# Shifting the copies of transposed probabilities by one slot and spreading the projections over the slots of a fused attention kernel

## The chip, the cores and the metric

The kernel runs on one core of a Trainium2 chip. The metric is device time in microseconds. The engines are TensorE (PE), VectorE (DVE), ScalarE (ACT), GpSimd (POOL) and the SP queue, which issues most DMAs. Each engine runs its own list of instructions in order and meets the others only at semaphores.

## What is computed

Sixteen images of 256 rows by 256 columns go through a small fixed filter and give 256 tokens each; 77 text tokens per image are looked up in a table, so that each batch item has S = 333 tokens of width 256. Two residual blocks follow, windowed attention with 16 heads of width 16 and a mixture of 8 experts with 2 chosen for each token:

```python
h = concatenate([filter(x), table[x_txt]], axis=1)            # [16, 333, 256]
h = h + attention(layernorm(h))   # windows of 128 at 0, 64, 128, 192 and 205, position bias
                                  # softmax, average over the windows that cover a token, Wo
h = h + experts(layernorm(h))     # softmax gate, top 2 of 8, SwiGLU of width 512, weighted sum
```

## The kernel before

The program has two stages. The first runs `run_steps` (L291): a step for each b from -2 to 17, and in it every engine runs the same Python loop `for k in range(G)` with G = 20 slots, that is 5 windows of 4 groups, a group being 4 heads. A step works at once on five batch items in different states (`has`, L310): attention of item b (`att`), the end of attention, output projection, gate and second layernorm of item b-1 (`tail`), expert places and scatter of item b-2 (`tail2`), projections of item b+1 (`proj`), image and text loads of item b+2 (`inp`). The second stage (`run_tiles`, L296) runs the experts over sorted tiles of rows; it starts when the first is over, and its code is the same before and after.

What each engine does in slot k of the first stage, in this order:

- TensorE (L1042 on): scores of group k (4 bf16 products, L1052); transposes of the probabilities of group k-3 (L1063); product with the values for group k-4 (8 instructions, L1079); in slots 0, 4, 8, 12, 16 the transposes of `raw` (L1089), the output rows of a window; in slots 2, 6, 10, 14, 18 the transposes of `ctx_q` (L1097). Then the other work of that slot: slot 0 transposes of the normalised input (L1108), slot 1 the prefix counts (L1115), slots 2 to 5 one projection of q or k each (L1132), slots 8 and 9 the output projection (L1030), slot 11 all three projections of v (L1037), slot 16 transposes of the normalised rows (L1163), slot 18 the gate (L1170).
- ScalarE (L633 on): four Exp of group k-1 (L640); the copy of the transposed probabilities of group k-2 out of PSUM into `probsT` (L653), for three groups in four; in slots 3, 7, ... the copy `raw` (L660); in slots 2, 6, ... the copy `head_out` (L667); last the evacuations of the projections: `xT` in slot 0 (L672), q and k in slots 2 to 5 (L684), `x2T` in slot 16 (L691).
- VectorE (L775 on): score plus bias with row minimum for group k (L783); in slots 3, 7, ... the copy of group k-2, whose number in its window is `DVE_G` (L792); in slots 1, 5, ... reciprocals and `ctx_q` (L804, L811); and small work of the layernorms, the gate, the bf16 parts of q and k (`part_high`, L757, `part_middle`, L764), v with bias (`add_v`, L771), residual (L889), normalise (L738), two bit masks of the image differences (L878).
- GpSimd (L517 on): image differences (L540, L552), their sum and clip (L544, L549), the window sums (L527), the remaining bf16 parts (L507, L514), six indirect stores (L498), inverse roots for the layernorms (`inverse_roots`, L473), copies and residual.
- SP (L334 on): for the next item, writes of the bf16 parts to DRAM and loads of them back as stacks (L365, L372), in one fixed order; then the shifts of v (L396 to L400), which wait for `add_v`; then the image loads of the next step (L342 to L346).

The buffers that couple the engines are two deep for `s_bank` (scores), `t_bank` (transposed probabilities in PSUM) and `probsT`, four deep for `probs`. TensorE's transposes into a `t_bank` buffer wait for the copy of two groups before (L1061). The projections share `m_bank`, so that the q and k products of one half wait for the evacuation of the product before in it (L1128).

## Time and profile before

| | |
|---|---|
| median of 3 runs | 1393.93 us (1393.73 to 1397.23) |
| profiled execution | 1392.94 us, span 1390.1 us |
| TensorE busy in the span | 1172.4 us (84%) |
| VectorE busy | 847.6 us (61%) |
| ScalarE busy | 710.9 us (51%) |
| GpSimd busy | 590.6 us (42%) |
| first stage with attention | about 60 to 830 us, 16 batch items |
| expert stage | about 870 to 1390 us |

Times in the profile are microseconds from the start of the span. A share of busy time over the whole span mixes the two stages, so the first stage is read by itself, in seven steps from 403.7 to 738.9 us in which every kind of work is present. An idle time is shown with the instruction that came after it and with the one that ended it.

### The profile page before, as it was taken

The page shows a single profiled execution, that of the slowest core. Times are in us where ns is not written, and L with a number is a line of the kernel's source. Part 1 is how long each engine was busy: PE and PEld are TensorE (multiplying, and loading weights), DVE is VectorE, ACT ScalarE, POOL GpSimd, SP SyncE. Part 2 cuts the span into 40 slices and gives each one's busy share as a digit, 9 for nine tenths or more (in the row PEclk, how much of TensorE's full clock was granted, in tenths as well). Part 3 has the DMA queues.
Part 4 walks back from the last instruction along what each step waited for, and adds up shares of the span by engine and source line. Part 5 has one row for each costly group of instructions (what it writes and reads, how often), then busy time and mean ns, then how long its engine had stood idle before and what let it go on. Part 6 is the DMA issues. An engine that isn't in the chain of part 4 may idle for free.

```text
span 1390.1 us, 34367 instructions
## 1 busy us (share of the span) xinstructions
PE 1172.4 (84%) x10510; PEld 964.1 (69%) x10511; DVE 847.6 (61%) x4259; ACT 710.9 (51%) x1976; POOL 590.6 (42%) x750
## 2 busy tenths in 40 slices
PE   1366888788888888888888872999999999999996
PEld 1244666566666666666666551999999999999995
DVE  4364777877777777878877764344444444444442
ACT  0185878877788788788778870211111111111111
POOL 5443365546546554654564334232322232223222
PEclk9698999999999999999999995999999999999998
DMA  3694464366336444633653307232232333232322
GB/s 111 148 240 92 98 146 88 88 126 131 78 94 141 102 88 111 146 80 86 136 122 64 86 28 229 38 51 46 49 47 48 49 45 49 46 49 46 49 45 34
DMA packets 98394, 123.31 MB, mean 89 GB/s; under 512 B 15544, under 2 KB 87416, under 8 KB 95192
## 3 DMA queue, kind: packets, MB, share of 16 engines
q1 hardware_dynamic: 75880, 89.96, 29.1%
q0 software_dynamic: 18576, 24.47, 10.9%
q10 hardware_dynamic: 3808, 7.34, 1.8%
q8 instruction: 59, 0.97, 0.3%
q14 instruction: 71, 0.58, 0.2%
HBM read 69.35 MB, written 46.07 MB: 83 GB/s over the span
## 4 chain that ended last, share of the span: by engine, by line
PE 65%; ACT 17%; DVE 6%; issue 6%; DMA 4%; POOL 2%; SPq 1%; another core or an unknown queue 0%; ACTq 0%; DVEq 0%; POOLq 0%
PE s_bank L1196 12%; PE t_bank L1196 12%; PE o_bank L1211 11%; ACT probs L640 8%; PE t_bank L1063 6%; PE m_bank L1132 4%; PE m_bank L1030 3%; DMA qk_parts<-parts_flat 3%; PE s_bank L1052 3%; PE o_bank L1089 3%; PE o_bank L1079 3%; PE m_bank L1037 3%; ACT raw L660 2%; ACT probsT L653 2%; DVE probs L783 1%
## 5 line engine op out<-in xcount | busy, mean ns | idle before, releaser
L640 ACT ACTIVATE probs<-probs,neg_max 128x128 f32<-128x128 f32 x1280 | 407.0, 397 | 6.9 <-DVE neg_max L783 6.8
L783 DVE CUSTOM_DVE_ANT_0 probs<-s_bank,nbias 128x128 f32<-128x128 f32 x1280 | 293.5, 285 | 72.2 <-PE s_bank L1052 68.1
L653 ACT ACTIVATE probsT<-t_bank 128x512 f32<-128x512 f32 x240 | 142.2, 593 | 136.4 <-PE t_bank L1063 122.4
L1063 PE MATMUL t_bank<-ident,probs 128*128 128x128 f32 x1280 | 203.8, 284 | 3.8 <-ACT probs L640 3.5
L705 ACT ACTIVATE v_all<-s_bank 128x512 f32<-128x512 f32 x91 | 54.4, 598 | 286.5 <-PE s_bank L1196 276.6
L1211 PE MATMUL o_bank<-stacks,v_all 128*128 x728 | 172.4, 380 | 0.6 <-issue 0.3
L1052 PE MATMUL s_bank<-stacks 96*128 96x128 bf16 x1280 | 130.9, 226 | 48.4 <-DMA stacks<-qk_parts 37.6
L1052 PEld LDWEIGHTS s_bank<-stacks 96*128 96x128 bf16 x1280 | 93.5, 101 | 94.2 <-DMA stacks<-qk_parts 38.3
L617 POOL DMA_INDIRECT out_dram<-wq_sb,nbias x46 | 74.8, 1627 | 193.1 <-DVE wq_sb L985 171.8
L617 POOL DMA_INDIRECT out_dram<-wk_sb,nbias x45 | 73.6, 1635 | 176.4 <-DVE wk_sb L985 173.6
L1063 PEld LDWEIGHTS t_bank<-ident,probs 128*128 128x128 f32 x1280 | 141.8, 147 | 7.1 <-ACT probs L640 7.0
L1079 PE MATMUL o_bank<-probsT,v_all 128*32 128x128 f32 x2560 | 139.5, 290 | 6.2 <-ACT head_out L667 5.7
L1211 PEld LDWEIGHTS o_bank<-stacks,v_all 128*128 128x128 f32 x728 | 131.3, 190 | 15.6 <-issue 1.5
L991 DVE TENSOR_TENSOR v_all<-v_all,t_bank 128x512 f32<-128x512 f32 x91 | 62.6, 688 | 128.6 <-PE t_bank L1196 128.6
L792 DVE COPY probsT<-t_bank 128x512 f32<-128x512 f32 x80 | 55.2, 691 | 105.1 <-PE t_bank L1063 104.6
L498 POOL DMA_INDIRECT expert_slots<-rows,slot_i x96 | 96.0, 1000 | 46.7 <-issue 38.2
L699 ACT ACTIVATE v_all<-m_bank 128x256 f32<-128x256 f32 x91 | 34.9, 383 | 143.0 <-PE m_bank L1185 143.0
L783 DVE DVE_READ_ACCUMULATOR2_ANT neg_max<- 128x1 f32 x1280 | 105.0, 82 | 0.0
L1089 PE MATMUL o_bank<-ident,raw 128*128 128x128 f32 x320 | 53.5, 290 | 55.7 <-ACT raw L660 55.4
L1079 PEld LDWEIGHTS o_bank<-probsT,v_all 128*32 128x32 f32 x2560 | 52.0, 109 | 64.0 <-issue 50.8
L1196 PEld LDWEIGHTS s_bank<-v_all,probs 128*128 128x128 f32 x736 | 91.0, 195 | 3.2 <-ACT v_all L699 0.9
L1196 PE MATMUL s_bank<-v_all,probs 128*128 128x128 f32 x736 | 91.4, 278 | 0.5 <-ACT v_all L699 0.5
(159 smaller groups left out, 2065.3 us busy)
## 6 DMA issues: line engine op xcount, KB each, us to landing
stacks<-qk_parts SPq DMA_DIRECT2D x192, 166.5 KB
qk_parts<-parts_flat SPq DMA_DIRECT2D x192, 83.2 KB
nbias<-expert_slots SPq DMA_DIRECT2D x91, 129.0 KB
w_sb<-in_L_ffn_w_dram ACTq DMA_DIRECT2D x14, 512.0 KB
v_all<-v_all SPq DMA_DIRECT2D x64, 96.0 KB, 3.4
x_here<-in_x_dram SPq DMA_DIRECT2D x16, 256.0 KB, 3.0
out_dram<-h_res SPq DMA_DIRECT2D x16, 256.0 KB
stacks<-in_L_ffn_w_dram SPq DMA_DIRECT2D x8, 512.0 KB
```

The source lines that it names most:

```text
L498: pool.indirect_dma_start(slots_dram[:, :], bass.IndirectOffsetOnAxis(slot_i[0:n, kk, j:j + 1], 0), rows[0:n, kk, j, :], None).then_inc(sc ...
L617: pool.indirect_dma_start(out[:, :], bass.IndirectOffsetOnAxis(g_rows[r][:, D + 1:D + 2].bitcast(I32), 0), y_sb[r], None, compute_op=ALU.a ...
L640: ins = act.activation(seg, seg, ACT.Exp, bias=neg_max[:, r, i:i + 1], scale=-1.0)
L653: act.activation(probsT[:, k % 2, :], t_bank[:, k % 2, :], ACT.Copy).then_inc(pT_by_act, 1)
L783: ins = dve.tensor_tensor_reduce(probs[:, r, i * WIN:(i + 1) * WIN], s_bank[:, k % 2, i * WIN:(i + 1) * WIN], nbias[:, h, :], 1.0, BIG, AL ...
L991: dve.tensor_tensor(hidT[r % 2], hidT[r % 2], t_bank[:, r % 2, :], ALU.mult).then_inc(hid_ready, 1)
L1052: mm = pe.matmul(s_bank[:, k % 2, i * WIN:(i + 1) * WIN], q_stack[par][0:KROWS, h, lo:lo + WIN], k_stack[par][0:KROWS, h, lo:lo + WIN], st ...
L1063: mm = pe.transpose(t_bank[:, (k - 3) % 2, i * WIN:(i + 1) * WIN], probs[:, r, i * WIN:(i + 1) * WIN], ident[:, :])
L1079: mm = pe.matmul(o_bank[32 * i:32 * i + 32, vp, g * WIN:(g + 1) * WIN], v_win[bp][:, w, c0:c0 + 2 * HD], probsT[:, (k - 4) % 2, i * WIN:(i ...
L1089: mm = pe.transpose(o_bank[:, vp, g * WIN:(g + 1) * WIN], raw[:, g * WIN:(g + 1) * WIN], ident[:, :])
L1196: mm = pe.matmul(bank[:, par, n * P:(n + 1) * P], up_w[par][:, m, a, n * P:(n + 1) * P], gxT[par][:, a * P:(a + 1) * P], start=(a == 0), s ...
L1211: mm = pe.matmul(o_bank[:, r % 2, 0:D], hidT[r % 2][:, a * P:(a + 1) * P], w2_sb[:, bass.ds(e, 1), a, :].rearrange("p o n -> p (o n)"), st ...
```

## The change

The copies of `probsT` move by one slot on ScalarE and VectorE: slot k now copies group k-3 instead of k-2, and VectorE's share is the group with number 3 of a window instead of 1, so that it copies in slots 2, 6, 10, 14, 18. TensorE's products with the values stay where they are. On TensorE the `raw` transposes go to the very end of their slot, the q and k projections are given out as six pieces over slots 2 to 6, the output projection over slots 8 to 10, the v projections over slots 11 to 14, the gate over slots 17 and 18, and the prefix counts go from slot 1 to 2. On ScalarE the evacuations stand first in a slot: `xT` in slot 1, q and k in slots 3, 4, 6, 7, `x2T` in slot 17. VectorE and GpSimd have their small work moved to fit: the second layernorm's statistics in slot 12, roots in 13, normalise in 15 (before: 11, 12, 14); `add_v` in 14 and 15 (12, 13); `part_high(1)` in slot 7 (6) and `part_middle(0)` in 6 (7); the image differences both in slot 0 (2, 3), both masks in slot 1 (2, 4), sum and clip in slot 2 (6).

```diff
-DVE_G = 1
+DVE_G = 3
...
-                    if inp and k == 2:
+                    if inp and k == 0:
...
                         pool.tensor_tensor(diag[:, :, :], x_here[:, :, 0:IMG], x_below[:, :, 1:IMG + 1],
                                            ALU.subtract).then_inc(diffs_ready, 1)
-                    if inp and k == 6:
+                    if inp and k == 0:
+                        pool.tensor_tensor(anti[:, :, :], x_below[:, :, 0:IMG], x_here[:, :, 1:IMG + 1],
+                                           ALU.subtract).then_inc(diffs_ready, 1)
+                    if inp and k == 2:
...
                         pool.tensor_tensor(diag[:, :, :], diag[:, :, :], anti[:, :, :], ALU.add).then_inc(conv_step, 1)
...
-                    if inp and k == 3:
-                        pool.tensor_tensor(anti[:, :, :], x_below[:, :, 0:IMG], x_here[:, :, 1:IMG + 1],
-                                           ALU.subtract).then_inc(diffs_ready, 1)
...
-                    if (tail or inp) and k == 12:
+                    if (tail or inp) and k == 13:
...
-                    if tail and k == 15:
+                    if tail and k == 16:
...
+                    if proj and k == 1:
+                        act.wait_ge(xT_done, b1 + 1)
+                        if b1 >= 1:
+                            act.wait_ge(v_done, b1 * 2)
+                        act.activation(xT[:, :, :], m_bank[:, :, 0:S], ACT.Copy).then_inc(xT_ready, 1)
+                    if proj and k in (3, 4, 6, 7):
+                        n, c = {3: (0, 0), 4: (0, 1), 6: (1, 0), 7: (1, 1)}[k]
+                        act.wait_ge(qk_done, b1 * 4 + 2 * n + c + 1)
+                        if b1 >= 1:
+                            act.wait_ge(rest_ready, b1 * 2)
+
+                        act.activation(qk[:, 2 * n + c, :], m_bank[:, c, 0:S], ACT.Identity,
+                                       bias=(bq_col if n == 0 else bk_col)[:, c:c + 1],
+                                       scale=(-SCALE if n == 0 else 1.0)).then_inc(qk_ready, 1)
+                    if tail and k == 17:
+                        act.wait_ge(x2T_done, b0 + 1)
+                        if proj:
+                            act.wait_ge(part3_ready, b1 * 2 + 2)
+                        act.activation(x2T[:, :, :], m_bank[:, :, 0:S], ACT.Copy).then_inc(x2T_ready, 1)
...
-                    g = (k - 2) % NG
-                    if g != DVE_G and ((k >= 2 and att) or (k < 2 and tail)):
-                        n = b * G + (k - 2)
+                    if (k - 3) % NG != DVE_G and ((k >= 3 and att) or (k < 3 and tail)):
+                        n, r = b * G + (k - 3), (k - 3) % 2
                         act.wait_ge(pT_done, n + 1)
                         if n >= 2:
                             act.wait_ge(pv_done, n - 1)
-                        act.activation(probsT[:, k % 2, :], t_bank[:, k % 2, :], ACT.Copy).then_inc(pT_by_act, 1)
+                        act.activation(probsT[:, r, :], t_bank[:, r, :], ACT.Copy).then_inc(pT_by_act, 1)
...
-                    if tail2 and k == 1:
+                    if tail2 and k == 2:
...
                         ins.then_inc(max_ready, 1)
-                    if (k - 2) % NG == DVE_G and ((k >= 2 and att) or (k < 2 and tail)):
-                        n = b * G + (k - 2)
+                    if (k - 3) % NG == DVE_G and ((k >= 3 and att) or (k < 3 and tail)):
+                        n, r = b * G + (k - 3), (k - 3) % 2
                         dve.wait_ge(pT_done, n + 1)
                         if n >= 2:
                             dve.wait_ge(pv_done, n - 1)
-                        dve.tensor_copy(probsT[:, k % 2, :], t_bank[:, k % 2, :]).then_inc(pT_by_dve, 1)
...
                     if proj and k == 6:
+                        part_middle(0)
+                    if proj and k == 7:
                         part_high(1)
-                    if proj and k == 7:
-                        part_middle(0)
-                    if inp and k in (2, 4):
-                        dve.wait_ge(diffs_ready, b2 * 2 + k // 2)
-                        bits = (diag, anti)[k // 2 - 1][:, :, :].bitcast(I32)
-                        dve.tensor_scalar(bits, bits, 0x7FFFFFFF, None, ALU.bitwise_and).then_inc(conv_step, 1)
+                    if inp and k == 1:
+                        for i, side in enumerate((diag, anti)):
+                            dve.wait_ge(diffs_ready, b2 * 2 + i + 1)
+                            bits = side[:, :, :].bitcast(I32)
+                            dve.tensor_scalar(bits, bits, 0x7FFFFFFF, None, ALU.bitwise_and).then_inc(conv_step, 1)
...
                         moments_of(h_in[par], stats1, 0, b2, ln1_step)
-                    if tail and k == 10:
-                        dve.wait_ge(wo_done, b0 * 2 + 2)
+                    if tail and k in (10, 11):
+                        dve.wait_ge(wo_done, b0 * 2 + k - 9)
                         dve.wait_ge(res_ready, b0 + 1)
...
-                    if tail and k == 11:
+                    if tail and k == 12:
...
-                    if proj and k == 12:
+                    if proj and k == 14:
...
-                    if proj and k == 13:
+                    if proj and k == 15:
                         add_v(2, 4)
-                    if tail and k == 14:
+                    if tail and k == 15:
...
+                def qk_proj(n, c, a):
+                    mm = pe.matmul(m_bank[:, c, 0:S], (wq_sb if n == 0 else wk_sb)[:, a, c * P:(c + 1) * P],
+                                   xT[:, a, :], start=(a == 0), stop=(a == C - 1))
+                    if a == C - 1:
+                        mm.then_inc(qk_done, 1)
+
+                def v_proj(bank, o, w, a):
+                    mm = pe.matmul(m_bank[:, bank, o:o + D], xT[:, a, STARTS[w]:STARTS[w] + WIN],
+                                   wv_sb[:, a, :], start=(a == 0), stop=(a == C - 1))
+                    if w and a == C - 1:
                         mm.then_inc(v_done, 1)
 
...
-                    v = (k - 5) // NG
-                    if (k - 5) % NG == 3 and ((att and v >= 0) or (tail and v < 0)):
...
+                    if tail2 and k == 2:
...
-                    if proj and k in (2, 3, 4, 5):
...
+                    if proj and k == 2:
+                        pe.wait_ge(xT_ready, b1 + 1)
+                        qk_proj(0, 0, 0)
+                        qk_proj(0, 0, 1)
+                    if proj and k == 3:
+                        if tail2:
                             pe.wait_ge(prefix_read, b9 * 2 + 2)
...
+                        qk_proj(0, 1, 0)
+                        qk_proj(0, 1, 1)
+                    if proj and k == 4:
+                        pe.wait_ge(qk_ready, b1 * 4 + 1)
+                        qk_proj(1, 0, 0)
+                    if proj and k == 5:
+                        qk_proj(1, 0, 1)
+                        pe.wait_ge(qk_ready, b1 * 4 + 2)
+                        qk_proj(1, 1, 0)
+                    if proj and k == 6:
+                        qk_proj(1, 1, 1)
...
                     if tail and k == 9:
                         out_proj(1)
+                    if tail and k == 10:
...
                     if proj and k == 11:
                         pe.wait_ge(qk_ready, b1 * 4 + 4)
                         if tail:
+                            pe.wait_ge(h2_ready, b0 * NT + 2)
+                        v_proj(0, 0, 0, 0)
+                        v_proj(0, 0, 0, 1)
+                    if proj and k == 12:
+                        v_proj(0, D, 2, 0)
+                    if proj and k == 13:
+                        v_proj(0, D, 2, 1)
+                        if tail:
                             pe.wait_ge(h2_ready, b0 * NT + NT)
-                        v_proj(0, 0, 0)
-                        v_proj(0, D, 2)
-                        v_proj(1, 0, 4)
+                        v_proj(1, 0, 4, 0)
+                    if proj and k == 14:
+                        v_proj(1, 0, 4, 1)
                     if tail and k == 16:
                         pe.wait_ge(rows0_ready, b0 * 3 + 3)
                         if proj:
...
-                    if tail and k == 18:
+                    if tail and k in (17, 18):
                         pe.wait_ge(x2T_ready, b0 + 1)
-                        for j, (t0, n) in enumerate(TILES):
+                        for j in ((0, 1), (2,))[k - 17]:
...
+                        if k == 18:
+                            mm.then_inc(logits_done, 1)
+                    v = (k - 5) // NG
+                    if (k - 5) % NG == 3 and ((att and v >= 0) or (tail and v < 0)):
+                        wv, vp = b * NW + v, (par + v) % 2
+                        pe.wait_ge(raw_ready, wv + 1)
+                        for g in range(NG):
+                            mm = pe.transpose(o_bank[:, vp, g * WIN:(g + 1) * WIN], raw[:, g * WIN:(g + 1) * WIN],
+                                              ident[:, :])
+                        mm.then_inc(rawT_done, 1)
```

## Rows read from the trace of the kernel before

**Rows 1.** Seven batches: busy us of PE, PEld, DVE, ACT, POOL (count), clock, DMA.

```profile
451.40:498.40 47.00, 39.69 (x421) 28.67 (x420) 37.72 (x246) 38.80 (x114) 26.55 (x38) 1.00 0.52 110
498.40:547.80 49.40, 42.74 (x421) 30.91 (x419) 37.58 (x242) 38.60 (x113) 26.44 (x38) 0.93 0.48 105
...
sum 335.20, PE 287.76 PEld 207.44 DVE 263.73 ACT 271.08 POOL 184.15; mean PE 41.11 PEld 29.63 DVE 37.68 ACT 38.73 POOL 26.31
```

**Rows 2.** Groups by line, 403.7 to 738.9 us: busy, mean ns, idle before, releasers.

```profile
L640 ACT ACTIVATE probs<-probs,neg_max 128x128 f32<-128x128 f32 x562 | 178.8, 397 | 3.7 <-DVE neg_max L783 3.7
L783 DVE CUSTOM_DVE_ANT_0 probs<-s_bank,nbias 128x128 f32<-128x128 f32 x563 | 129.2, 285 | 21.5 <-PE s_bank L1052 20.9 <-issue 0.4
...
L653 ACT ACTIVATE probsT<-t_bank 128x512 f32<-128x512 f32 x105 | 62.3, 593 | 53.9 <-PE t_bank L1063 49.4 <-issue 2.8 <-remote 1.5
...
L1052 PE MATMUL s_bank<-stacks 96*128 96x128 bf16 x560 | 57.5, 227 | 5.8 <-DVE neg_max L783 5.8
...
L1089 PE MATMUL o_bank<-ident,raw 128*128 128x128 f32 x142 | 23.8, 290 | 22.2 <-ACT raw L660 22.1
L1079 PEld LDWEIGHTS o_bank<-probsT,v_all 128*32 128x32 f32 x1120 | 22.7, 109 | 27.7 <-issue 22.5 <-ACT probsT L653 5.2
...
L1097 PE MATMUL o_bank<-ident,ctx_q 128*128 128x128 f32 x70 | 16.6, 321 | 7.6 <-DVE ctx_q L811 7.6
```

**Rows 3.** Waits, 403.7 to 738.9 us: who waited for whom, total, times, longest.

```profile
PE m_bank L1115 <- ACT xT L672: 7.3, 7, 1.0
```

**Rows 4.** Chain around slot 16 of one batch: start us, us, what.

```profile
488.81 0.60 ACT raw L660
...
490.92 0.44 PE t_bank L1063 x4
```

**Rows 5.** Timeline of ScalarE, 489 to 540 us: start us, us, operation, idle before.

```profile
491.89 0.72 ACT L691 ACTIVATE rest<-m_bank 128x666 f32<-128x666 f32 x1
...
520.98 0.60 ACT L653 ACTIVATE probsT<-t_bank 128x512 f32<-128x512 f32 x1 [2.75 <-issue]
```

**Rows 6.** Timeline of TensorE, 480 to 545 us: start us, us, operation, idle before.

```profile
494.15 0.39 PE L1052 MATMUL s_bank<-stacks 96*128 96x128 bf16 x4
...
494.91 0.43 PE L1079 MATMUL o_bank<-probsT,v_all 128*32 128x128 f32 x8
495.26 0.40 PE L1052 MATMUL s_bank<-stacks 96*128 96x128 bf16 x4
...
525.75 2.83 PE L1037 MATMUL m_bank<-wv_sb,xT 128*128 128x256 f32 x12
...
539.38 0.74 PE L1163 MATMUL m_bank<-ident,rows 128*128 128x128 f32 x6
...
544.69 0.40 PE L1052 MATMUL s_bank<-stacks 96*128 96x128 bf16 x4
```

**Rows 7.** Timeline of VectorE, 521.9 to 548 us: the normalise of slot 14.

```profile
535.35 1.06 DVE L738 TENSOR_SCALAR rows<-h_res,moments,rstd 128x256 f32<-128x256 f32 x3
```

**Rows 8.** Timeline of GpSimd, 489 to 541 us: a difference, the last root step.

```profile
498.27 1.10 POOL L540 TENSOR_TENSOR diag<-x_here,x_below 128x512 f32<-128x512 f32 x1
...
535.02 0.20 POOL L489 TENSOR_TENSOR rstd<-rstd,root_tmp 128x6 f32<-128x6 f32 x1
```

**Rows 9.** VectorE's L818 over the span: ns min/median/max, first and last start.

```profile
L818 DVE TENSOR_TENSOR below_best<-best x16: 178/954/990, 163.4 to 852.5; 128x24 f32<-128x24 f32 x16
```

**Rows 10.** Chain of the first attention batch: start us, us, what.

```profile
87.01 14.14 DMA qk_parts<-parts_flat
...
114.02 0.61 PE s_bank L1052 x4
```

**Rows 11.** Timeline of SP's queue, 490 to 600 us: last stack load, next image.

```profile
533.72 0.31 SPq L372 DMA_DIRECT2D stacks<-qk_parts  x1
...
538.76 0.44 SPq L345 DMA_DIRECT2D x_below<-in_x_dram  x1
```

**Rows 12.** The page's part 6: DMA issues, KB each, us to landing.

```profile
x_here<-in_x_dram SPq DMA_DIRECT2D x16, 256.0 KB, 3.0
```

More of the change, by code:

```diff
@@ L791, in step @@
                             dve.wait_ge(pv_done, n - 1)
-                        dve.tensor_copy(probsT[:, k % 2, :], t_bank[:, k % 2, :]).then_inc(pT_by_dve, 1)
+                        dve.tensor_copy(probsT[:, r, :], t_bank[:, r, :]).then_inc(pT_by_dve, 1)
                     v = (k - 6) // NG
@@ L1033, in out_proj @@
                         mm.then_inc(wo_done, 1)
-                def v_proj(bank, o, w):
-                    for a in range(C):
-                        mm = pe.matmul(m_bank[:, bank, o:o + D], xT[:, a, STARTS[w]:STARTS[w] + WIN],
-                                       wv_sb[:, a, :], start=(a == 0), stop=(a == C - 1))
-                    if w:
+                def qk_proj(n, c, a):
[7 more added lines that the diff above has]
+                    if w and a == C - 1:
                         mm.then_inc(v_done, 1)
@@ L1083, in step @@
                         mm.then_inc(pv_done, 1)
-                    v = (k - 5) // NG
-                    if (k - 5) % NG == 3 and ((att and v >= 0) or (tail and v < 0)):
-                        wv, vp = b * NW + v, (par + v) % 2
-                        pe.wait_ge(raw_ready, wv + 1)
-                        for g in range(NG):
-                            mm = pe.transpose(o_bank[:, vp, g * WIN:(g + 1) * WIN], raw[:, g * WIN:(g + 1) * WIN],
-                                              ident[:, :])
-                        mm.then_inc(rawT_done, 1)
+                    if tail2 and k == 2:
+                        pe.wait_ge(taken_ready, b9 + 1)
+                        if proj:
+                            pe.wait_ge(xT_ready, b1 + 1)
+                        pe.matmul(counted[:, 0:NT * E], before[:, :], taken[:, :, :].rearrange("p j e -> p (j e)"),
+                                  start=True, stop=False, skip_group_check=True)
+                        for j in range(NT):
+                            mm = pe.matmul(counted[:, (j + 1) * E:(NT + 1) * E].rearrange("p (r e) -> p r e", e=E),
+                                           ones[:, :], taken[:, j:j + 1, :].to_broadcast([P, NT - j, E]),
+                                           start=False, stop=(j == NT - 1), skip_group_check=True)
+                        mm.then_inc(prefix_done, 1)
                     v = (k - 7) // NG
@@ L1109, in step @@
                         mm.then_inc(xT_done, 1)
-                    if tail2 and k == 1:
-                        pe.wait_ge(taken_ready, b9 + 1)
-                        if proj:
-                            pe.wait_ge(xT_ready, b1 + 1)
-                        pe.matmul(counted[:, 0:NT * E], before[:, :], taken[:, :, :].rearrange("p j e -> p (j e)"),
-                                  start=True, stop=False, skip_group_check=True)
-                        for j in range(NT):
-                            mm = pe.matmul(counted[:, (j + 1) * E:(NT + 1) * E].rearrange("p (r e) -> p r e", e=E),
-                                           ones[:, :], taken[:, j:j + 1, :].to_broadcast([P, NT - j, E]),
-                                           start=False, stop=(j == NT - 1), skip_group_check=True)
-                        mm.then_inc(prefix_done, 1)
@@ L1123, in step @@
[L1123 to L1134 removed]
+                    if proj and k == 2:
+                        pe.wait_ge(xT_ready, b1 + 1)
+                        qk_proj(0, 0, 0)
+                        qk_proj(0, 0, 1)
@@ L1171, in step @@
                                                start=(a == 0), stop=(a == C - 1))
-                        mm.then_inc(logits_done, 1)
+                        if k == 18:
[8 more added lines that the diff above has]
+                        mm.then_inc(rawT_done, 1)
             run_steps(step)
```

32 lines of the change are left out of this document (3 added, 29 removed).

## Prediction

> **What bounds the kernel now.** I read the table of engines by stretch first, for the attention stage alone. Over seven batches of 335.2 us in all, 47.9 us a batch, TensorE is busy 41.1 us, ScalarE 38.7 and VectorE 37.7 [rows 1]. No engine is full: TensorE idles 6.8 us a batch, ScalarE 9.2, VectorE 10.2. Three engines with nearly equal loads run in lists that are coupled through two-deep buffers, and what is lost is lost in waits for each other, so the kernel is bound by the order of work and not by one engine. A batch has 20 slots, 2.4 us each on average. A slot with attention work alone starts 1.11 us after the one before on TensorE, while slot 11 carries 2.83 us of v projections at once [rows 6]. ScalarE's four Exp and a copy take 318 x 4 + 593 ns = 1.87 us at most (178.8 us over 562 Exp is 318 ns) in every slot [rows 2]. So TensorE waits in the bare slots and ScalarE in the full ones, because only about one slot of work fits between them.
>
> The groups by line then say where TensorE waits in these seven batches: 22.2 us before the `raw` transposes (L1089), 7.6 us before the `ctx_q` transposes (L1097), 5.8 us before the scores (L1052) [rows 2], and 7.3 us before the prefix counts, for `xT` [rows 3]. ScalarE waits 53.9 us before its copies of `probsT`, nearly all for the transposes of L1063 [rows 2].
>
> The chain shows that the two are one loop. ScalarE issues `raw` at 488.81 us (0.60 us), TensorE stands until that is done, then does the `raw` transposes, the six transposes of slot 16, scores, and only then the transposes that end at 491.36 [rows 4], for which ScalarE's next copy was waiting. ScalarE has had 1.2 us of Exp to do in between and idles for the rest. Slots 0, 4, 8 and 16 have such a stretch of other work behind the `raw` transposes; in slot 8 of that batch ScalarE idled 2.75 us [rows 5].
>
> **The change, part by part.** The batch is the unit; gains and losses are in us a batch.
>
> `raw` transposes last in their slot. They now stand behind 0.45 to 1.0 us of projections or transposes, and ScalarE issues `raw` right behind the copy for which the product of L1079 waits. The wait of 22.2 / 7 = 3.17 goes [rows 2]. What is late next: `ctx_q` on VectorE a slot later, which has TensorE's whole next slot as cover.
>
> `xT` evacuated in slot 1 and first used in slot 2, prefix counts in slot 2. The wait of 7.3 / 7 = 1.04 goes [rows 3]. ScalarE now waits for transposes that TensorE did at the end of the slot before; its copy of that slot (593 ns) covers most of them.
>
> Projections spread. The 2.83 us of slot 11 [rows 6] become pieces over four slots, and statistics, residual and `add_v` on VectorE are spread too. The waits for VectorE (L1097 and L1052) are (7.6 + 5.8) / 7 = 1.9 [rows 2]. They come from bunches of small work, of which the change undoes some and makes one new. I count half, 0.96; bounds 0 and 1.9. Sum of gains 3.17 + 1.04 + 0.96 = 5.17.
>
> Copies one slot later. Between TensorE and ScalarE the loop stays one slot long: before, slot k of ScalarE needed transposes of slot k+1 and fed the product of slot k+2; now those of slot k, for the product of slot k+1. What is gained is that the transposes no longer wait for the Exp right behind the copy. What is lost is a slot between scores and product: Exp of group k now has to be over before the copy of group k-2. ScalarE's waits turn into waits of TensorE before L1079. Today TensorE's weight loads there wait 5.2 / 7 = 0.74 for the copy [rows 2]. In the bare slots (1, 7, 15, 19) ScalarE is the slower engine, so part of the 3.17 has to come back. Bounds: 0 and the whole 3.17. I take 1.1, nearer the 0.74, since that is the same wait.
>
> Normalise one slot later (slot 15), used by TensorE in slot 16. Today it starts at 535.35, lasts 1.06 us and ends 3.0 us before the transposes of 539.38 [rows 6, 7]; the last root step ends at 535.22 [rows 8], so it can't start earlier relative to the statistics. A slot is 2.4 us, so 0.6 us of cover is left on average. Loss between 0 and 1.06; I take 0.3.
>
> Gate from slot 17 on. `x2T` (0.72 us, [rows 5]) now stands first in ScalarE's slot 17 and TensorE's gate of the same slot needs it; TensorE has only the product of L1079 (0.35 us from 494.91 to 495.26, [rows 6]) beside it. Loss 0.72 - 0.35 = 0.4, bounds 0 and 0.72.
>
> VectorE's slots 0 to 2. They hold the choice of experts, both masks and now the copy of `probsT`, and GpSimd's two image differences stand beside them. A small VectorE operation on 128x24 values (L818) takes 954 ns in the median against 178 at least; it starts at the time of GpSimd's 1.10 us difference [rows 8, 9]. With two differences in a row a second operation can be held up in that way: bounds 0 and 2 x 0.78 = 1.6 for the slowest chain; I take 0.6, since part of it hides behind ScalarE. The image itself must be there by slot 0: its load follows the shifts of v in SP's queue, which wait for `add_v`, now two slots later. Today it is issued by 538.76 and lands 3.0 us later [rows 11, 12], 2.9 us ahead of the next step's first scores at 544.69 [rows 6]; two slots (4.8 us) later it lands 1.9 us behind them. GpSimd then waits, and VectorE's masks of slot 1 after two differences (2.2 us). VectorE's slots 0 and 1 cover about 4 us of it, so I cost it at nothing; uncovered it would be up to 2 us a batch.
>
> In sentences of its own: the Trainium skill, "SBUF — State Buffer", section "Who interferes with whom", says that a VectorE instruction with two SBUF inputs contends with a GpSimd instruction that reads SBUF, and that the later one is blocked until the first is done. By that rule the trace's 954 ns is such a block, and it speaks against putting both differences next to the choice of experts; what it would cost is a rival below.
>
> Sum of losses 1.1 + 0.3 + 0.4 + 0.6 = 2.4; net gain 5.17 - 2.4 = 2.77 a batch.
>
> The q and k chain to DRAM starts its second half two slots later (`part_high(1)`), and the write that needs it stands in SP's queue ahead of the stack loads. In the steady state the last stack load is issued at 533.72 for scores at 544.69 [rows 6, 11], 11 us of cover for 4.8, so it costs nothing. In the first batch there is no cover: the chain runs through DMA waits of up to 14.14 us and TensorE stands until 114.02 [rows 10]. I take 2.5 us of loss once, bounds 0 and 4.8.
>
> Sum. Items 1 to 14 have all the work: 14 x 2.77 = 38.8. The last item has no projections behind its `raw` transposes; 0.5. The first gives -2.5. The expert stage isn't touched. 38.8 + 0.5 - 2.5 = 36.8, and the profiled execution of 1392.94 us becomes 1356.1; it lies 1 us under the median of 1393.93, so I forecast 1356. TensorE's clock is left as it is: batches with a granted clock of 1.00 take 47.0 us and one with 0.93 takes 49.4 [rows 1], and I can't say which way fewer and shorter waits push it.
>
> **The rivals.**
> 1. Spreading works fully. Gains with the whole of VectorE's waits (6.1), losses as above (2.4), and every batch at clock 1.00 (47.0 in place of 47.9, 0.9): 4.6 a batch, 14 x 4.6 + 0.5 - 2.5 = 62.4, 1331 us. For it: loads of 38 to 41 us allow batches near 43. Against: three engines in lists rarely run without waits.
> 2. The blocks on VectorE bite. The two L818-like delays show in full (1.6 in place of 0.6): 1.77 a batch, 1370 us. It is what the rule of the skill above gives, though worked out from rows 8 and 9.
> 3. The waits only change their name. TensorE stands before L1079 for as long as it stood before L1089 (3.17 in place of 1.1): 0.70 a batch, 1385 us. For it: ScalarE is the slower engine in the bare slots, whatever TensorE's order.
> 4. Slower: the shortened path from scores to product. From the end of scores k-1 to the product of slot k+1 TensorE has, in bare slots, 2 x 1.11 + 0.76 - 0.22 = 2.76 us [rows 6]. In that time stand VectorE's minimum (129.2 us over 141 groups, 0.92), four Exp (1.27), the copy (0.59) [rows 2] and now an evacuation ahead of them (up to 0.72, [rows 5]): 3.5 us, 0.74 too long. In the six slots with under 0.5 us of projections that is 4.4 a batch; 2.77 - 4.4 = -1.7, and 14 x 1.7 + 2 = 26 us of loss, 1418 us. It decides from 0.46 us in each of the six slots. Against it: the Exp of slot k is mostly ahead of need, since ScalarE idles 9.2 us a batch, and only three of the evacuations fall beside such slots.
>
> **How the numbers follow.** Forecast 0.43 (own range 1345 to 1366), rival 1 0.17, rival 2 0.14, rival 3 0.14, rival 4 0.12. The range of 8 in 10 is 1328 to 1390: it holds the forecast and rivals 1 to 3 with the lower bounds of the unknown costs, and leaves out rival 4 and the far side of rival 1. A change under 0.3% (4 us) can't be told from none here. Faster by more: 0.43 + 0.17 + 0.14 and most of rival 3, 0.83; within 0.3%: 0.05, from rival 3; slower: 0.12.
>
> **What would show it.** In the profile after, the idle time before L1089 should be near zero and that before the prefix counts gone; idle time before L1079 shows the share that came back (1.1 a batch or 3). The transposes of slot 16 should wait little for the normalise, the gate about 0.4 us for `x2T`. VectorE's masks should not wait for the differences for long. A batch should be 45.1 us, from one `xT` transpose to the next; the first item's stack loads should end by some 2 us later. I am wrong if TensorE's idle time before L1079 grows to 3 us or more, if scores wait more for VectorE than the 0.83 of now, or if GpSimd waits for the image and VectorE with it.

## The result and the profile after

The changed kernel takes 1339.16 us in the median (1335.66 to 1344.43) against 1393.93 us, 0.9605 of the time before with a 95% interval of 0.9567 to 0.9642. It is faster, as forecast, by 54.8 us where 38 were forecast (1356 us).

The table by stretch of seven batches of the changed kernel; columns as in [rows 1]:

```profile
379.60:424.10 44.50, 39.50 (x422) 28.44 (x418) 38.35 (x241) 38.78 (x113) 26.34 (x38) 1.00 0.54 122
...
467.90:512.20 44.30, 39.57 (x424) 28.46 (x419) 38.27 (x244) 38.95 (x114) 26.14 (x38) 1.00 0.53 121
...
sum 309.70, PE 276.89 PEld 199.00 DVE 268.36 ACT 271.97 POOL 185.08; mean PE 39.56 PEld 28.43 DVE 38.34 ACT 38.85 POOL 26.44
```

A batch takes 309.7 / 7 = 44.2 us, not 47.9. ScalarE's load is the same (38.9 us) and VectorE's hardly more (38.3). TensorE is busy 39.6 us instead of 41.1, with a granted clock of 1.00 in all seven batches, where five of the seven before had 0.96 and one 0.93, and it idles 4.7 us instead of 6.8.

The groups by line over these seven batches, with the same columns as [rows 2]; L671 is the copy that was L653, L1085 the product with the values (L1079), L1193 the raw transposes (L1089), L1108 the `ctx_q` transposes (L1097), L1058 the scores (L1052), L1176 the transposes of slot 16:

```profile
L671 ACT ACTIVATE probsT<-t_bank 128x512 f32<-128x512 f32 x105 | 61.1, 582 | 0.1
L1085 PE MATMUL o_bank<-probsT,v_all 128*32 128x128 f32 x1124 | 59.9, 285 | 21.2 <-ACT probsT L671 11.2 <-DVE probsT L791 9.4
...
L1058 PE MATMUL s_bank<-stacks 96*128 96x128 bf16 x560 | 54.8, 219 | 0.3 <-DMA stacks<-qk_parts 0.2
...
L1193 PE MATMUL o_bank<-ident,raw 128*128 128x128 f32 x140 | 21.1, 273 | 0.8 <-issue 0.8
...
L1108 PE MATMUL o_bank<-ident,ctx_q 128*128 128x128 f32 x70 | 15.2, 298 | 2.5 <-DVE ctx_q L810 2.5
...
L1176 PE MATMUL m_bank<-ident,rows 128*128 128x128 f32 (+1 forms) x42 | 5.6, 268 | 8.1 <-DVE rows L737 8.1
...
L1095 PE MATMUL m_bank<-taken,before 128*128 128x24 bf16 x7 | 1.3, 187 | 0.0
```

The reader should see three things. ScalarE no longer waits for transposes: 0.1 us before its copies where it was 53.9. TensorE no longer waits before the raw transposes (0.8 us, was 22.2) or the prefix counts (L1095, 0.0, was 7.3). And it waits in two new places: 21.2 us before the product with the values, for copies of ScalarE and of VectorE, and 8.1 us before the transposes of slot 16, for the normalise.

The gain is made batch by batch. The transposes of the normalised input mark each batch on TensorE. First the kernel before, then the changed one (start us, us, operation):

```profile
163.31 0.74 PE L1108 MATMUL m_bank<-ident,xn 128*128 128x128 f32 x6
```

```profile
738.95 0.74 PE L1108 MATMUL m_bank<-ident,xn 128*128 128x128 f32 x6
```

```profile
157.94 0.80 PE L1119 MATMUL m_bank<-ident,xn 128*128 128x128 f32 x6
```

```profile
689.31 0.80 PE L1119 MATMUL m_bank<-ident,xn 128*128 128x128 f32 x6
```

Twelve batches lie between each pair: 575.6 us before, 531.4 after, 3.69 us less a batch. That is 44.3 of the 54.7 us by which the two spans differ (1390.1 and 1335.4). The rest is 5.4 us up to the first mark and 5.1 behind the last, of which 4.0 lie in the last two items; the expert stage takes 519.4 us, and 520.4 before.

### The profile page after: what moved, and what is told of

It reads as the page before. It is cut to its first block, busy times and chain, and to the rows that moved or that the text cites. A ratio compares the mean times of both kernels' runs of the same rounds, so it can differ in the third digit from the quotient of the medians.

```text
span 1335.4 us, 34370 instructions
## 1 busy us (share of the span) xinstructions
PE 1153.5 (86%) x10510; PEld 948.7 (71%) x10511; DVE 856.0 (64%) x4259; ACT 712.9 (53%) x1976; POOL 588.7 (44%) x750
## 4 chain that ended last, share of the span: by engine, by line
PE 50%; DMA 15%; DVE 9%; issue 8%; SPq 6%; POOL 5%; ACT 3%; another core or an unknown queue 0%; POOLq 0%; DVEq 0%; ACTq 0%
PE s_bank L1219 12%; PE t_bank L1219 12%; PE o_bank L1234 12%; DMA qk_parts<-parts_flat 10%; PE m_bank L1037 4%; DMA out_dram<-h_res 4%; SPq L372 3%; DVE probs L782 2%; SPq L365 2%; PE o_bank L1085 2%; PE t_bank L1069 2%; PE m_bank L1208 2%; POOL h_res L606 1%; ACT probs L659 1%; PE s_bank L1058 1%
## 5 line engine op out<-in xcount | busy, mean ns | idle before, releaser
L1069 PE MATMUL t_bank<-ident,probs 128*128 128x128 f32 x1280 | 194.8, 275 | 0.0
L1085 PE MATMUL o_bank<-probsT,v_all 128*32 128x128 f32 x2560 | 136.7, 286 | 47.3 <-ACT probsT L671 28.6
L1058 PE MATMUL s_bank<-stacks 96*128 96x128 bf16 x1280 | 126.7, 221 | 36.9 <-DMA stacks<-qk_parts 35.2
L1058 PEld LDWEIGHTS s_bank<-stacks 96*128 96x128 bf16 x1280 | 94.2, 100 | 81.0 <-DMA stacks<-qk_parts 37.8
L671 ACT ACTIVATE probsT<-t_bank 128x512 f32<-128x512 f32 x240 | 139.8, 583 | 17.2 <-PE t_bank L1069 15.9
L1069 PEld LDWEIGHTS t_bank<-ident,probs 128*128 128x128 f32 x1280 | 135.3, 142 | 0.4 <-issue 0.4
L1085 PEld LDWEIGHTS o_bank<-probsT,v_all 128*32 128x32 f32 x2560 | 50.4, 108 | 107.5 <-ACT probsT L671 52.9
L498 POOL DMA_INDIRECT expert_slots<-rows,slot_i x96 | 96.0, 1000 | 52.3 <-issue 43.8
L782 DVE DVE_READ_ACCUMULATOR2_ANT neg_max<- 128x1 f32 x1280 | 108.9, 88 | 0.0
L1219 PE MATMUL t_bank<-v_all,probs 128*128 128x128 f32 x736 | 89.7, 275 | 0.0
L1219 PEld LDWEIGHTS s_bank<-v_all,parts_flat 128*128 128x128 f32 x720 | 87.4, 192 | 3.0 <-ACT v_all L698 0.7
```

The costliest lines, as they stand in the source:

```text
L498: pool.indirect_dma_start(slots_dram[:, :], bass.IndirectOffsetOnAxis(slot_i[0:n, kk, j:j + 1], 0), rows[0:n, kk, j, :], None).then_inc(sc ...
L671: act.activation(probsT[:, r, :], t_bank[:, r, :], ACT.Copy).then_inc(pT_by_act, 1)
L782: ins = dve.tensor_tensor_reduce(probs[:, r, i * WIN:(i + 1) * WIN], s_bank[:, k % 2, i * WIN:(i + 1) * WIN], nbias[:, h, :], 1.0, BIG, AL ...
L1058: mm = pe.matmul(s_bank[:, k % 2, i * WIN:(i + 1) * WIN], q_stack[par][0:KROWS, h, lo:lo + WIN], k_stack[par][0:KROWS, h, lo:lo + WIN], st ...
L1069: mm = pe.transpose(t_bank[:, (k - 3) % 2, i * WIN:(i + 1) * WIN], probs[:, r, i * WIN:(i + 1) * WIN], ident[:, :])
L1085: mm = pe.matmul(o_bank[32 * i:32 * i + 32, vp, g * WIN:(g + 1) * WIN], v_win[bp][:, w, c0:c0 + 2 * HD], probsT[:, (k - 4) % 2, i * WIN:(i ...
```

## Experiments

**Theory 1**: the place of the raw transposes is what pays. **Theory 2**: the later copies pay. **Theory 3**: spreading the projections pays. In the prediction the first had 3.17 us of gain, the third 0.96, and the second was a loss. Four kernels tell them apart, each edit alone on the kernel before or undone alone in the changed one.

**Raw transposes last, alone.** Kernel before, with the block moved to the end of TensorE's slot:

```diff
                         mm.then_inc(pv_done, 1)
-                    v = (k - 5) // NG
-                    if (k - 5) % NG == 3 and ((att and v >= 0) or (tail and v < 0)):
...
                         mm.then_inc(logits_done, 1)
+                    v = (k - 5) // NG
+                    if (k - 5) % NG == 3 and ((att and v >= 0) or (tail and v < 0)):
```

> The kernel before with one edit: the raw transposes stand at the very end of their slot, as in the changed kernel; copies, projections, evacuations and small work as before. Theory 1 (the place of the raw transposes is what pays, since it opens the loop raw - raw transposes - other products - transposes - copy): the 3.2 us a batch before L1089 go and half comes back elsewhere, the clock rises to 0.98 or more; 1345 to 1360 us. Theory 2 (the later copies are what pays, since they let ScalarE issue raw right behind a copy it does not wait for): 1380 to 1392 us. Theory 3 (spreading the projections pays): 1380 to 1392 us too.

Measured: 1357.6 us, ratio 0.9706 (0.968 to 0.9732). The edit by itself pays three quarters of what the whole change pays, in the range that theory 1 gave for it, though the clock of this run is 0.957 and not 0.98. ScalarE still waits for transposes:

```profile
L653 ACT ACTIVATE probsT<-t_bank 128x512 f32<-128x512 f32 x105 | 62.2, 593 | 47.9 <-PE t_bank L1063 47.5
...
L1170 PE MATMUL o_bank<-ident,raw 128*128 128x128 f32 x140 | 22.6, 286 | 1.9 <-ACT raw L660 1.9
```

**Copies one slot later, alone.** Kernel before, with

```diff
-DVE_G = 1
+DVE_G = 3
-                    if g != DVE_G and ((k >= 2 and att) or (k < 2 and tail)):
-                        n = b * G + (k - 2)
+                    if (k - 3) % NG != DVE_G and ((k >= 3 and att) or (k < 3 and tail)):
+                        n, r = b * G + (k - 3), (k - 3) % 2
```

and the same on VectorE.

> The kernel before with one edit: the copies of transposed probabilities one slot later, VectorE's share is group 3; everything else as before. Theory 1: ScalarE's wait for transposes shrinks, but TensorE still stands before the raw transposes in five slots; 1375 to 1392 us, clock below 0.98. Theory 2: 1345 to 1365 us, wait before the raw transposes under 1 us a batch. Theory 3: 1380 to 1394 us.

Measured: 1341.83 us, ratio 0.9605 (0.9578 to 0.9632), which is the ratio of the whole change. Theory 2 stands. Theory 1 was wrong about this kernel: the raw transposes stay where they were, and TensorE doesn't wait for them. Its table and groups over seven batches:

```profile
469.90:514.20 44.30, 40.84 (x420) 29.34 (x419) 39.32 (x242) 38.78 (x113) 26.64 (x38) 0.96 0.52 117
...
sum 310.00, PE 285.53 PEld 205.08 DVE 270.24 ACT 271.14 POOL 183.88; mean PE 40.79 PEld 29.30 DVE 38.60 ACT 38.73 POOL 26.27
```

```profile
L1078 PE MATMUL o_bank<-probsT,v_all 128*32 128x128 f32 x1120 | 62.4, 297 | 18.8 <-ACT probsT L652 14.8 <-DVE probsT L791 3.8
L652 ACT ACTIVATE probsT<-t_bank 128x512 f32<-128x512 f32 x106 | 61.7, 582 | 13.9 <-PE t_bank L1062 13.9
...
L1088 PE MATMUL o_bank<-ident,raw 128*128 128x128 f32 x142 | 23.5, 288 | 0.8
```

TensorE waits 0.8 us before the raw transposes (L1088), as in the changed kernel, and ScalarE 13.9 us before its copies, where it was 53.9. A batch is 44.3 us long, again as there, though the granted clock is 0.96 and TensorE is busy 1.2 us a batch longer (40.8 against 39.6).

That doesn't make the clock worth nothing. The same trace has three earlier batches at a granted clock of 1.00, from 117.28 to 247.27 us, and they take 43.00, 43.05 and 43.94 us. One of them:

```profile
160.28:203.33 43.05, 39.45 (x420) 28.46 (x419) 38.12 (x244) 38.46 (x114) 25.92 (x38) 1.00 0.55 121
```

In the kernel before a batch at 1.00 takes 46.9 us (the next one in [rows 1] is of 0.93 and takes 49.4). So at either clock the late copies alone take about 3.5 us off a batch: 46.9 to 43.3 at 1.00, 47.8 to 44.3 at 0.96. The changed kernel takes 44.3 us at 1.00, the mean of the twelve batches above, 1.0 us more than the late copies alone at that clock (0.7 more than the 43.6 of eight batches at 1.00 in the kernel with late copies and the old share, further below). By these rows its other edits cost something, and its better clock gives that back. No run sets the clock apart from the order of work, so why it is 1.00 there stays open.

**The raw transposes back in their old place, in the changed kernel.**

> The changed kernel with one edit undone: the raw transposes again right behind the product with the values, ahead of the projections of their slot. Theory 1: a wait of 0.2 to 1.1 us before L1089 in five slots a batch comes back; 1350 to 1380 us. Theory 2: raw is issued right behind the copy that the product waits for, so only 0.1 to 0.2 us a window; 1339 to 1352 us. Theory 3: 1339 to 1350 us.

Measured: 1335.33 us, ratio 0.9546 (0.9507 to 0.9586). Undoing this edit costs nothing, as theory 2 said. TensorE's wait for the normalise falls from 8.1 to 2.0 us in seven batches, and it waits elsewhere instead, 7.1 us of it for the stack loads.

**The copies back in their old slot, in the changed kernel**, with VectorE's share at group 1 again.

> The changed kernel with one edit undone: the copies of transposed probabilities in the slot before (group k-2, VectorE's share group 1 again). Theory 1: 1335 to 1350 us, and the waits of TensorE before L1085 (3.0 us a batch in the changed kernel) get smaller. Theory 2: 1375 to 1392 us, ScalarE waits for transposes again, 5 us a batch or more. Theory 3: 1340 to 1355 us.

Measured: 1415.02 us, ratio 1.0117 (1.0083 to 1.0152), slower than the kernel before by 1.2% and beyond what any theory expected. With early copies, all the other edits together bring no time and cost some. ScalarE's wait is back, larger than before the change, and VectorE's work comes late:

```profile
L672 ACT ACTIVATE probsT<-t_bank 128x512 f32<-128x512 f32 x105 | 62.5, 596 | 68.1 <-PE t_bank L1070 68.0
...
L1109 PE MATMUL o_bank<-ident,ctx_q 128*128 128x128 f32 x70 | 16.3, 317 | 12.2 <-DVE ctx_q L811 12.2
...
L1177 PE MATMUL m_bank<-ident,rows 128*128 128x128 f32 (+1 forms) x42 | 6.5, 300 | 12.5 <-DVE rows L738 12.5
```

68.1 / 7 = 9.7 us a batch before ScalarE's copies, and in seven batches 12.2 us before the `ctx_q` transposes and 12.5 before those of slot 16. The clock falls too, and batches of one kernel differ by it:

```profile
362.30:415.63 53.33, 45.72 (x419) 32.34 (x419) 40.48 (x243) 39.72 (x115) 27.32 (x38) 0.87 0.43 97
415.63:461.04 45.41, 39.85 (x418) 28.47 (x419) 38.38 (x243) 37.81 (x111) 25.36 (x37) 1.00 0.50 114
```

Of the 7.9 us between these two batches 5.9 are TensorE's busy time. Four of 13 batches in this trace have a clock of 1.00 and take 45.4 to 46.1 us, less than the 46.9 of the kernel before at that clock; the other nine have 0.85 to 0.93 and take 48.3 to 53.9. So the loss is in batches of low clock. Their waits are longer as well, and which came first is not shown.

**Both, on the kernel before.** If the two edits open one loop, they don't add.

> The kernel before with the later copies and with the raw transposes last in their slot. Later copies alone gave 0.9605 of the time before, raw transposes last alone 0.9706. If both open the same loop: no gain on top, 1336 to 1350 us. If they act on different losses: 1300 to 1320 us.

Measured: 1336.69 us, ratio 0.9588 (0.9556 to 0.9619): no gain on top of the copies that can be told from the noise. That fits one loop that either edit opens and the copies open further.

**Slot or share?** The later copies change two things, the slot and the group that VectorE takes. The share alone:

```diff
-DVE_G = 1
+DVE_G = 3
```

> The kernel before with VectorE's share of the copies changed alone (group 3 of a window in place of group 1, so slots 1, 5, 9 in place of 3, 7, 11); copies still in the early slot. If the gain of the later copies is their slot: 1385 to 1405 us, since now ScalarE copies in the slots in which it issues raw, and raw comes later. If it is the share: 1345 to 1365 us.

Measured: 1528.1 us, ratio 1.0943 (1.0892 to 1.0993), much slower than expected. The timeline of TensorE (start us, us, operation, idle before) has the same wait in every window:

```profile
406.63 0.68 PE L1097 MATMUL o_bank<-ident,ctx_q 128*128 128x128 f32 x2 [1.14 <-DVE ctx_q L811]
...
420.33 0.44 PE L1097 MATMUL o_bank<-ident,ctx_q 128*128 128x128 f32 x2 [1.14 <-DVE ctx_q L811]
...
424.53 0.66 PE L1089 MATMUL o_bank<-ident,raw 128*128 128x128 f32 x4 [1.61 <-ACT raw L660]
```

VectorE's early copy now falls into the slots 1, 5, 9, ahead of the reciprocals and `ctx_q` in VectorE's list, and waits there for transposes of TensorE's next slot. In that same next slot TensorE needs `ctx_q`. So 1.14 us before the `ctx_q` transposes and 0.6 to 1.6 before the raw ones come in every window from 400 to 460 us. The counterpart, the late slot with the old share:

> The kernel before with the later copies, but VectorE's share left at group 1 of a window (so it copies in slots 0, 4, 8). Group 3 in the early slot gave 1.094 of the time before, group 3 in the late slot 0.9605. If the late slot pays by itself, and the share only has to keep off the slots of the raw copy: 1340 to 1360 us. If the gain needs group 3 (raw, which follows the product of group 3, then waits for VectorE's copy of that group and not for ScalarE's own): 1375 to 1410 us.

Measured: 1335.89 us, ratio 0.9587 (0.9571 to 0.9603). The late slot pays by itself, with either share.

**Spreading the v projections on top of late copies** (slots 11 to 14, additions in 14 and 15, as in the change):

> The kernel before with the later copies, and the v projections spread over slots 11 to 14 with their additions in slots 14 and 15; everything else as before. If spreading pays once the copies are late: 1325 to 1335 us. If it doesn't (slots have elastic enough coupling then): within 5 us of the 1342 us that the later copies alone gave.

Measured: 1344.39 us, ratio 0.9636 (0.9611 to 0.9662). Spreading them brings nothing. Spreading the rest (q, k, output projection, gate) wasn't tried by itself.

**What is left in the changed kernel.** Theory A: the two new waits that have a cause of their own, the late image and the late normalise, are losses. Theory B: ScalarE would make TensorE wait there anyway. Three kernels. Image loads early, in SP's queue:

```diff
-                if inp:
-                    if b2 >= 1:
-                        sp.wait_ge(diffs_ready, b2 * 2)
...
+                    if b2 + 1 < B:
+                        load_image(b2 + 1)
                     sp.wait_ge(v_ready, b1 * 3 + 3)
```

> The changed kernel, with the image and text loads of the next step issued in SP's queue ahead of the wait for v and its four shifts, and not behind them; nothing else. Theory A (the late image is a loss: GpSimd waits for the indices, VectorE 1.6 us for the difference, TensorE 1.3 us a batch for VectorE's copy in slot 3): VectorE's wait for the differences goes, 1318 to 1330 us. Theory B (ScalarE, 39 of 44 us busy, is the bound, and the wait only changes its name): 1333 to 1341 us.

Measured: 1337.81 us, ratio 0.9605 (0.9577 to 0.9633): nothing gained. Statistics and roots in slots 11 and 12:

```diff
-                    if tail and k == 12:
+                    if tail and k == 11:
...
-                    if (tail or inp) and k == 13:
+                    if (tail or inp) and k == 12:
```

> The changed kernel, with the statistics of the second layernorm in slot 11 and the roots in slot 12, as before the change, while the normalise stays in slot 15. Theory A (TensorE's 1.16 us a batch for the normalise is a loss of its own, and comes from statistics and roots and not from the slot of the normalise): that wait goes, 1320 to 1330 us. Theory B (it is only standing that ScalarE would cause a moment later): the wait before the product with the values grows by as much, 1334 to 1341 us.

Measured: 1338.34 us, ratio 0.9611 (0.9566 to 0.9655): nothing gained. Both:

> Both edits together, image loads early and statistics and roots a slot earlier. Theory A: both gains add, 1302 to 1318 us. Theory B: 1330 to 1340 us.

Measured: 1326.15 us, ratio 0.9502 (0.9477 to 0.9527). Each alone brings nothing and both together bring 13 us, so neither theory holds. The single edits show where the first went. With early statistics alone the wait for the normalise falls only to 4.7 us over 306 us. Over the same stretch the changed kernel with early images (its traced execution took 1331.22 us, 6.6 less than its median):

```profile
L1090 PE MATMUL o_bank<-probsT,v_all 128*32 128x128 f32 x1104 | 58.8, 285 | 10.8 <-ACT probsT L676 9.5 <-DVE probsT L796 0.6
...
L1113 PE MATMUL o_bank<-ident,ctx_q 128*128 128x128 f32 x70 | 15.7, 308 | 8.4 <-DVE ctx_q L815 8.4
...
L1181 PE MATMUL m_bank<-ident,rows 128*128 128x128 f32 (+1 forms) x42 | 5.6, 268 | 8.3 <-DVE rows L742 8.3
```

TensorE's wait before the product (L1090) is half of what it was, 10.8 us, and the part of it for VectorE's copy nearly gone. But it now waits 8.4 us before the `ctx_q` transposes (L1113), which was 2.5, and 8.3 for the normalise (L1181), as before. With both edits these two are 5.2 and 4.9:

```profile
L1113 PE MATMUL o_bank<-ident,ctx_q 128*128 128x128 f32 x70 | 15.5, 304 | 5.2 <-DVE ctx_q L815 5.2
...
L1181 PE MATMUL m_bank<-ident,rows 128*128 128x128 f32 (+1 forms) x42 | 5.6, 268 | 4.9 <-DVE rows L742 4.9
```

Both are waits for VectorE, at other points of its list. The likely account is that with one cause taken away TensorE came earlier to the next. The clock has a share that isn't settled: of twelve batches between the marks two to three in each of these three traces have a granted clock of 0.96 and take 45.5 to 47.5 us, and the others, at 1.00, take 43.8 us in the mean with early images, 43.9 with early statistics and 43.1 with both, against 44.3 in the changed kernel, whose twelve are all at 1.00. At that clock each edit alone gains a little.

**The fastest.** The same with the raw transposes in their old place:

> The changed kernel with image loads early, statistics and roots a slot earlier, and the raw transposes again right behind the product with the values. If the end of the slot brings nothing once the copies are late, as the two earlier runs say: 1312 to 1328 us, the fastest so far or equal to it. If the place matters once the other waits are gone: 1330 to 1340 us.

Measured: 1322.26 us, ratio 0.9469 (0.9439 to 0.9499), faster than the changed kernel by 1.3% and than the kernel before by 5.3%. Against the 1326.15 us with the raw transposes last the difference is within the intervals.

## Why the prediction was right or wrong

The direction and the range were right, the size was a third too small, and the reason given for most of it was wrong. That the sum came as near as it did is luck. Its largest gain isn't due to the edit that it was given to, its largest loss is the edit that pays by itself, and the two errors went opposite ways. At an equal clock of 1.00 a batch went from 46.9 to 44.3 us, 2.7 less, where the sum had 2.77; the rest of the 3.69 goes with the clock, which the sum left as it was.

- *Raw transposes last, 3.17 gained.* The wait went (0.8 / 7 = 0.1 us a batch is left), but not because of this edit: it goes as well with the transposes in their old place and late copies. The loop was seen rightly in [rows 4]: raw, raw transposes, other products, transposes, copy. The step that failed was to ask only which of its members the change moves on TensorE. The late copy takes transposes that TensorE has made before the raw ones, one slot earlier in its list, and opens the loop from the other side. With early copies the edit does pay by itself (1357.6 us), but on top of late ones it brings nothing.
- *Copies one slot later, a loss of 1.1.* The prediction called this the part that costs. Alone it is worth 56 us (1341.83 against 1398.07 of the kernel before in the same comparison), 3.5 us a batch at an equal clock. The wait before the product did grow, from 0.4 us a batch (2.5 us in seven, the row below) to 21.2 / 7 = 3.0; 1.6 of it is for ScalarE and 1.3 for VectorE's copies. The sum of 1.1 and 0.6 was too small for that, and the gain on the other side was left out. The row of the kernel before, groups by line over the stretch of [rows 2]:

```profile
L1079 PE MATMUL o_bank<-probsT,v_all 128*32 128x128 f32 x1120 | 61.2, 291 | 2.5 <-ACT head_out L667 2.5
```
- *Spreading, 0.96 gained.* The waits before L1108 and L1058 fell from 1.9 to 0.4 us a batch. Where spreading of v was tried by itself, on top of late copies, it brought nothing.
- *`xT` in slot 1, 1.04 gained.* The wait before the prefix counts is gone. Which edit did it wasn't tried alone.
- *Normalise, 0.3 lost.* It is 8.1 / 7 = 1.16 a batch, above the upper bound of 1.06: not only the normalise but the statistics ahead of it moved by a slot, and the roots between them take 3.9 us whatever the slot length is. The prediction had said that the roots allow no earlier start, and then took an average slot as if the cover were elastic.
- *Gate, 0.4 lost.* No wait shows before it. "First in slot 17" and "last in slot 16" are the same place in ScalarE's list; only the copies moved past it. And the scores and transposes of slot 17 stand ahead of the gate beside the product, which the prediction counted alone: in the batch whose row transposes start at 505.06 us these end at 505.86, and the gate starts at 507.25, 1.39 us later, for 0.73 of `x2T`. With the copies early again the gate does wait, 6.2 us in seven batches.
- *Late image, nothing lost.* GpSimd waits 14.9 us in seven batches for the text indices, VectorE's masks wait 11.3 for the differences behind them, and a slot later TensorE waits 9.4 for VectorE's copy. That is 1.3 us a batch of TensorE's waiting, which the prediction gave as up to 2 if uncovered. Taken away alone it brings nothing, together with the statistics 13 us.
- *First item, 2.5 lost.* The second item's scores start at 113.60 us, and at 114.02 before [rows 10]. The write of the second half is issued 3.3 us later, and the DMA waits behind it are shorter. The issue in the chain of the kernel before, and then the chain of the changed kernel, with the columns of [rows 10]:

```profile
75.21 0.57 SPq L365
```

```profile
78.54 0.57 SPq L365
...
88.70 13.71 DMA qk_parts<-parts_flat
...
103.39 5.98 DMA qk_parts<-parts_flat
```

- *TensorE's clock, left out.* By these rows it is the term that was missing from the size. The forecast had it as it was; it went to 1.00 in all twelve batches between the marks, and the batches of one kernel put that at 0.9 to 1.0 us against 0.96 (47.8 and 46.9 before, 44.3 and a mean of 43.3 with late copies alone). Rival 1 had 0.9 for it. What raised the clock isn't shown.

Two of the signs named for being wrong came out: TensorE's wait before the product is 3.03 us a batch, just above 3, and GpSimd waits for the image's text indices and VectorE with it. Scores wait 0.04 us a batch, where 0.83 was the mark.

Rival 4, the shortened path from scores to product, didn't occur as a loss, though some of it is there: 8.6 us of waiting before ScalarE's Exp in seven batches, where it was 3.7. Rival 3 named the right place, the wait before the product, but it brought back 2.7 of the 3.2 us and the batch got shorter all the same, because ScalarE stopped waiting. Rival 2, the blocks on VectorE, exists at other lines (see the last section): one of 0.88 us lies ahead of the copy for which TensorE waits 1.3 us a batch. What it costs by itself wasn't tried. The gain stands between the forecast and rival 1.

## What to carry to other kernels

When engines run in-order lists that are coupled through two-deep buffers, write down for every wait which slot of the other engine it needs, and look for the loop that goes through one engine twice. Here a copy that takes what the producer made in the same slot, in place of the next one, cost a wait before the product and removed larger ones elsewhere, and it is worth all the time that a rewrite of the schedule brought. Compare batches at an equal clock as well as totals: two kernels with equal batches may owe them to different things. And an item that is moved must be judged by its neighbours in each engine's list and not by its slot number: the same share of work was 0.96 in one slot and 1.09 in the next.

## What the runs showed of the hardware that was not expected

VectorE's small operations are held up by GpSimd's work beside them, and the delay moves with the neighbours. The operation of [rows 9] fell from 954 ns in the median to 178, since GpSimd's differences no longer stand beside it. The mask of the first difference now runs beside the second difference. A cast of 128x6 values took 172 ns in the median before and takes 980 now; in one batch it runs from 476.79 to 477.77 us, beside a window sum of GpSimd (476.43 to 477.15) and the memset behind it, which ends at 477.74. Count, ns min/median/max, first and last start in the changed kernel:

```profile
L817 DVE TENSOR_TENSOR below_best<-best x16: 177/178/525, 158.5 to 798.0; 128x24 f32<-128x24 f32 x16
```

```profile
L878 DVE TENSOR_SCALAR diag<-diag x16: 414/1296/1302, 13.3 to 650.1; 128x512 int32<-128x512 int32 x16
L878 DVE TENSOR_SCALAR anti<-anti x16: 414/414/416, 14.4 to 651.3; 128x512 int32<-128x512 int32 x16
```

```profile
L867 DVE CAST slot_i<-slot_f x16: 172/980/984, 167.0 to 800.2; 128x6 int32<-128x6 f32 x16
```

Two masks of the same shape take 1296 and 414 ns in the median; the first starts while GpSimd's second difference runs, and ends 0.31 us behind it (474.08 and 473.77). The Trainium skill, "SBUF — State Buffer", section "Who interferes with whom", has this as a lock between the two engines that is held for a whole instruction. For a VectorE operation with one input in SBUF, as the mask and the cast are, it names only the two-port modes, and no trace here shows the mode. The times agree with such a lock for the mask, which takes 0.88 us more than its 0.41.

The granted clock differs from batch to batch of one kernel, and the time of a batch with it: 46.9, 47.8 and 49.4 us at 1.00, 0.96 and 0.93 in the kernel before, with no wait of TensorE longer than 1.2 us in these batches. A batch took 44.3 us both in the changed kernel at 1.00 and with late copies alone at 0.96, where it took 43.0 to 43.9 at 1.00.
